# Second expert product of a four-layer network as seven half-size block products, with 32x64 tiles for the attention scores

## The chip, the cores and the metric

The kernel runs on one core of a Trainium2 chip. Its engines work side by side: PE (TensorE: matmuls, with PEld its weight loads), DVE (VectorE), ACT (ScalarE), POOL (GpSimd), and the queue SP, which here starts nearly all DMAs. Each follows its own instruction list in order, and they wait for each other on semaphores. The metric is device time in microseconds (us) of one execution; smaller is better.

## What is computed

Eight images (B = 8) of 512 tokens with 256 channels go through four layers. Each adds `s * silu(g)` to the running `x`, where `s` is an attention-like part and `g` a feed-forward part. Layer 0 has causal attention with 16 heads, layer 3 has two attentions, of which the second (over all tokens, 16 heads) uses the same class as layer 0's. In layer 1, which takes nearly half of the time, `s` is a state-space part with a convolution of four taps, and `g` a mixture of eight experts, all of them computed for every token:

```python
zxbcdt = u @ W_in.T                      # z, xBC, dt
xBC = silu(conv(xBC) + conv_b)           # four taps over time
y, _ = ssd(x * dt[..., None], A * dt, Bm, Cm, CHUNK)
y = (y + x * D).reshape(b, L, D_INNER) * silu(z)
s = rmsnorm(y) * norm_w @ W_out.T

gates = entmax_bisect(xt @ Wr + br)      # per token and expert
h = relu(einsum('td,edf->etf', xt, W1) + b1[:, None, :])   # 256 -> 1024
y = einsum('etf,efd->etd', h, W2) + b2[:, None, :]         # 1024 -> 256
g = silu(einsum('etd,te->td', y, gates))
```

All matmuls run in float32. The profile shows each of them as two records of a weight load and a matmul, one after the other.

## The kernel before

**Layer 1** (`layer1`, L967 on) goes over the 8 images and in each over 8 experts. For one expert the first product (`expert_in`) turns x into `hidden` (eight tiles of 128 features by 512 tokens). It is already done as seven block products of half size instead of eight (`PRODUCTS`, seven pairs of a bank "a" or "b" and a turn), 4 matmuls each with 256 moving columns, over four PSUM banks `hid`. The sums of weight blocks that this needs (`w1_sums`, S1 to S4) are made by POOL in `weight_sums`, the sums of inputs in `input_sums`, and ACT and DVE put the seven results together in `hidden` (`part_out`, `add_11`, `add_22`, `add_12`, `relus`). The second product (`expert_out`, L1203) is plain: for each of four token tiles j, eight matmuls add up over f into one of two banks `exp_out`, with 128 tokens of `hidden` as the stationary side and 256 columns of `w2` as the moving one, and DVE adds the result times the gate to `moe` (`expert_sum`, L1744). So an expert costs 56 records in `expert_in` and 64 in `expert_out`.

PE's order in an image is written by hand (`sequence`): the projections z0 to z3 and xb0 to xb3 (L1304), `expert_in(0)`, `expert_in(1)`, the gates, `expert_out(0)`, then `expert_in(e + 1)` and `expert_out(e)` in turn, with the state-space part in pieces between them (`cumulative`, `tokens`, `chunk_scores`, `chunk_products`), then `output` (L1296) and `expert_out(7)`. The projections and the state-space part share a ring of two banks, in the order of `names`; a bank can be written again when the engine that reads it is done (`Jobs.open` waits for `emptied`). ACT empties z0 to z3 (silu, L1428) and xb0 to xb3 (copy, L1364).

SP loads for every expert two halves of its first weights (`w1_first`, `w1_second`, 512 KB each) and its second weights (`w2`, 1 MB). `w1_second` and `w2` have two buffers each, so that load e + 2 starts when expert e is done with its own; `w1_first` has one.

**Attention** (class `Attention`, L285, used in layers 0 and 3): 16 heads, four at a time, each in its own 32 rows of the array. Every head's scores are computed twice, once for the row maxima (`score`, L387) and once transposed for the exponentials (`score_t`, L394), one matmul of 32 rows x 128 columns of weights for a tile of 128. `values` (L409) multiplies with four 128x32 tiles side by side. In a step PE runs score_t 0 and 1 and score 2 and 3, then the values, then score 0 and 1 and score_t 2 and 3. There are 128 steps in each of the two layers, with two such blocks of four score matmuls in each, so 512 blocks. In layer 0 a matmul has 512, 384, 256 or 128 moving columns (causal), in layer 3 always 512.

## Time and profile before

| | |
|---|---|
| median of 3 runs | 4200.58 us (4198.15 to 4203.7) |
| the profiled execution, its own time | 4203.91 us |
| its span in the trace | 4202.1 us |
| PE busy | 4062.9 us, 97% |
| PEld, DVE, ACT, POOL busy | 65%, 56%, 45%, 15% |
| mean granted TensorE clock | 0.986 of full |

A row of a timeline reads: start, length, engine, source line, operation, tile written and tiles read, shapes and count; in brackets how long the engine had been idle and who released it. A shape such as 32*128 is the weights' rows*columns, the shape after it what moves. A matmul's end is modelled, so the distance from start to start tells more than its length does. POOL, DVE, ACT and PE stand for the engines, SPq for the DMA queue of SP.

### The profile page before, as it was taken

The numbers are of one execution on the slowest core, as the hardware profiler recorded it, in microseconds if no ns is written. First come the engines' busy times: TensorE is split into PE (matmuls) and PEld (weight loads), VectorE is DVE, ScalarE is ACT, GpSimd is POOL, SyncE is SP. The second block draws the span as 40 slices with busy tenths as digits, with TensorE's granted clock in tenths as the row PEclk, the third lists the DMA queues.
The fourth block names the chain that finished last, engine by engine and source line by source line (L and its number), as shares of the span: only waits on it lengthen the run. The fifth ranks groups of instructions, "written<-read, shape, count | busy, mean of one in ns | idle before, by whom it ended". The sixth has DMA issues, their size and how long they took to land. (4 is left out here: it accounts for less than half of the span.)

```text
span 4202.1 us, 57679 instructions
## 1 busy us (share of the span) xinstructions
PE 4062.9 (97%) x21117; PEld 2729.2 (65%) x21117; DVE 2345.7 (56%) x4792; ACT 1888.4 (45%) x3783; POOL 646.7 (15%) x700
## 2 busy tenths in 40 slices
PE   7999999999999999999999999999998998999999
PEld 3444457888888888888888888666665554333333
DVE  6566655334343443434343343577777987667665
ACT  2454455435354444435444353455543221555555
POOL 0122123313133131323213131000000000000000
PEclk8999999999999999999999999999999999999999
DMA  3110102212122221222212121100000001011110
GB/s 90 17 17 16 34 12 99 80 61 98 65 85 79 71 88 61 88 71 87 82 61 88 66 97 47 47 1 1 1 1 22 1 1 26 16 24 21 26 24 22
DMA packets 61888, 198.51 MB, mean 47 GB/s; under 512 B 11257, under 2 KB 21121, under 8 KB 52745
## 3 DMA queue, kind: packets, MB, share of 16 engines
q1 hardware_dynamic: 60784, 194.55, 14.9%
q8 instruction: 172, 2.82, 0.3%
q14 instruction: 116, 0.94, 0.1%
q10 hardware_dynamic: 816, 0.20, 0.0%
HBM read 171.11 MB, written 4.46 MB: 42 GB/s over the span
## 5 line engine op out<-in xcount | busy, mean ns | idle before, releaser
L1211 PE MATMUL l_exp_out<-l_w,l_hidden 128*128 128x256 f32 x4096 | 913.6, 381 | 0.3
L1211 PEld LDWEIGHTS l_exp_out<-l_w,l_hidden 128*128 128x128 f32 x4096 | 769.0, 190 | 116.0 <-issue 9.1
L1369 ACT ACTIVATE l_hidden<-l_hid 128x512 f32<-128x512 f32 x384 | 227.7, 596 | 605.3 <-PE l_hid L1171 604.1
L1747 DVE SCALAR_TENSOR_TENSOR l_moe<-l_exp_out,l_gates,l_moe 128x256 f32<-128x256 f32 x256 | 123.8, 483 | 610.1 <-PE l_exp_out L1211 607.9
L1678 DVE TENSOR_TENSOR l_hidden<-l_hid,l_hidden 128x512 f32<-128x512 f32 x384 | 264.7, 691 | 348.2 <-PE l_hid L1171 343.7
L507 DVE TENSOR_REDUCE l3f_row_max<-l3f_bank 128x1 f32<-128x512 f32 x512 | 327.9, 685 | 176.9 <-PE l3f_bank L387 176.5
L463 ACT ACTIVATE l3f_prob_t<-l3f_bank 128x512 f32<-128x512 f32 x512 | 277.2, 596 | 206.1 <-PE l3f_bank L394 206.0
L1171 PE MATMUL l_hid<-l_x_sums,l_w_sums 128*128 128x256 f32 x1536 | 344.1, 381 | 7.4 <-DVE l_hidden L1678 7.4
L1171 PEld LDWEIGHTS l_hid<-l_x_sums,l_w_sums 128*128 128x128 f32 x1536 | 292.6, 191 | 47.6 <-issue 7.8
L504 DVE CUSTOM_DVE_ANT_0 l_masked<-l_bank,l_mask 128x256 f32<-128x256 f32 (+3 forms) x512 | 226.7, 487 | 161.0 <-PE l_bank L387 160.1
L1381 ACT ACTIVATE l_hidden<-l_hidden,l_w 128x256 f32<-128x256 f32 (+1 forms) x512 | 279.1, 605 | 65.2 <-DVE l_hidden L1678 64.8
L394 PE MATMUL l3f_bank<-l3f_qk_t 32*128 32x512 f32 x1024 | 302.9, 637 | 1.0 <-DMA l3f_qk_t<-l3f_set_rows 0.5
L387 PE MATMUL l3f_bank<-l3f_qk_t 32*128 32x512 f32 x1024 | 297.3, 643 | 5.4 <-DMA l3f_qk_t<-l3f_packed 5.2
L463 ACT ACTIVATE l_prob_t<-l_bank 128x256 f32<-128x256 f32 (+3 forms) x512 | 194.6, 436 | 208.4 <-PE l_bank L394 203.9
L1568 POOL TENSOR_TENSOR l_w_sums<-l_w_first,l_w_second 128x512 f32<-128x512 f32 x64 | 81.3, 1270 | 1116.4 <-PE l_hid L1171 1002.4
L394 PE MATMUL l_bank<-l_qk_t 32*128 32x512 f32 (+3 forms) x1024 | 217.8, 480 | 9.0 <-ACT l_prob_t L463 8.0
L387 PE MATMUL l_bank<-l_qk_t 32*128 32x512 f32 (+3 forms) x1024 | 217.1, 491 | 6.3 <-DMA l_qk_t<-in_alibi 5.5
L494 POOL TENSOR_SCALAR_AFFINE_SELECT l_prob_t<-l_prob_t 128x256 f32<-128x256 f32 x256 | 116.6, 457 | 502.0 <-ACT l_prob_t L463 501.6
L387 PEld LDWEIGHTS l3f_bank<-l3f_qk_t 32*128 32x128 f32 x1024 | 83.7, 183 | 97.5 <-issue 78.4
L409 PE MATMUL l3f_bank<-l3f_prob_t,l3f_v_ones 128*32 128x512 f32 x1024 | 138.1, 605 | 0.0
L394 PEld LDWEIGHTS l_bank<-l_qk_t 32*128 32x128 f32 x1024 | 92.1, 183 | 69.0 <-issue 44.7
L394 PEld LDWEIGHTS l3f_bank<-l3f_qk_t 32*128 32x128 f32 x1024 | 87.6, 183 | 75.1 <-issue 54.3
(525 smaller groups left out, 6779.3 us busy)
## 6 DMA issues: line engine op xcount, KB each, us to landing
l_w<-in_w SPq DMA_DIRECT2D x64, 1024.0 KB, 4.8
l_w_first<-in_w SPq DMA_DIRECT2D x64, 512.0 KB
l_w_second<-in_w SPq DMA_DIRECT2D x64, 512.0 KB, 3.7
l_mix<-l_cum SPq DMA_DIRECT2D x32, 512.0 KB, 4.8
l_qk_t<-l_packed SPq DMA_DIRECT2D x128, 64.0 KB
l3f_qk_t<-l3f_packed SPq DMA_DIRECT2D x128, 64.0 KB
all_x<-in_x SPq DMA_DIRECT2D x8, 512.0 KB, 6.0
out_x<-all_x SPq DMA_DIRECT2D x7, 512.0 KB, 3.0
```

Of the source, the lines that this page charges most:

```text
L387: flow.fill(nc.tensor.matmul(bank[:, 0:keys], self.q_t[rows, g, qt * P:(qt + 1) * P], self.k_t[rows, g, 0:keys], start=True, stop=True), ( ...
L394: flow.fill(nc.tensor.matmul(bank[:, 0:T - q.start], self.k_t[rows, g, kb * P:(kb + 1) * P], self.q_t[rows, g, q], start=True, stop=True), ...
L409: ins = nc.tensor.matmul(bank[self.rows(s), q], self.v[:, b % 2, kb, g * HPG + s, :], self.prob_t[:, u % (self.LAG + 1), s, 0:T - q.start] ...
L463: flow.empty(nc.scalar.activation(self.prob_t[:, t % (self.LAG + 1), s, 0:T - q.start], bank[:, 0:T - q.start], ACT.Exp), ("t", t, s))
L504: ins = nc.vector.tensor_tensor_reduce(self.masked[:, flow.index(("s", w, s)), 0:keys], bank[:, 0:keys], mask[:, T - keys:T], 1.0, NEG, AL ...
L507: ins = nc.vector.tensor_reduce(out, bank[:, 0:keys], AX, ALU.max)
L1171: ins = nc.tensor.matmul(bank[:, i * TH:(i + 1) * TH], weights[:, k * P:(k + 1) * P], moving, start=i == 0 and (which, turn) in (("a", 0), ...
L1211: ins = nc.tensor.matmul(bank[:, 0:C], hidden[:, e % 2, f, j * P:(j + 1) * P], w2[:, e % 2, f, :], start=f == 0, stop=f == HF - 1)
L1369: hid.empty(nc.scalar.activation(hidden_block(e, half_f, x, half_t), pair(bank), ACT.Copy), (e, x, which, turn))
L1381: return nc.scalar.activation(out, source, ACT.Relu, bias=w[:, B1][:, e * HF + k:e * HF + k + 1])
L1678: hid.empty(V.tensor_tensor(cell, pair(bank), cell, ALU.add), (e, x, which, turn))
L1747: exp_out.empty(V.scalar_tensor_tensor(moe[:, j, :], bank[:, 0:C], gates[:, j, e:e + 1], moe[:, j, :], ALU.mult, ALU.add), (e, j))
```

## The change

The second product of an expert now is seven block products too. Tokens, features and output columns are each cut in two; a product is 8 matmuls (2 token tiles x 4 feature tiles), still with 128 tokens of `hidden` stationary but with 128 moving columns of `w2`. Four sums of blocks of `w2` (R1, the one written over `w2_quarter(0, 1)`, R2, R4) are made by POOL (`w2_weight_sums`), four of `hidden` by DVE (`hidden_sum_1` to `hidden_sum_4`, one over `hidden_quarter(e, 1, 0)`, one over `hidden_quarter(e, 0, 1)`). The products go in turn to the two banks `exp_out` (a, b, a, b, a, b, a); some add to what the bank holds, and DVE adds each bank's state to `moe` after every product, so 14 operations of 128x128 for an expert take the place of 4 of 128x256.

`w1_second` and `w2` have one buffer now. The next expert's halves are loaded when the present expert is done with them, S3 is the first of the sums of `w1`, and S1, S2, S4 wait for the second half. The projections run xb0 to xb3 before z0 to z3. The convolution on DVE moves from `expert_out(0)` to the beginning of the image, among the additions of `expert_in(0)`. On ACT, Sqrt of the routing, Silu of `moe` and Exp and Ln of dt come between and behind the copies of xb and ahead of z. The routing is cut in pieces between the sums of expert 7.

In both attentions a score tile is computed as two matmuls of 32 rows x 64 columns of weights, into partitions 0 to 63 and 64 to 127 of the same bank, each with the same moving columns as before.

```diff
-            flow.fill(nc.tensor.matmul(bank[:, 0:keys], self.q_t[rows, g, qt * P:(qt + 1) * P], self.k_t[rows, g, 0:keys],
-                                       start=True, stop=True), ("s", w, s))
+            for m in range(0, P, 2 * SLOT):
+                ins = nc.tensor.matmul(bank[m:m + 2 * SLOT, 0:keys], self.q_t[rows, g, qt * P + m:qt * P + m + 2 * SLOT], self.k_t[rows, g, 0:keys],
+                                       start=True, stop=True)
+            flow.fill(ins, ("s", w, s))
...
-        w1_first, w1_second, w1_sums = a.sb("w1_first", [P, F]), a.sb("w1_second", [P, 2, F]), a.sb("w1_sums", [P, 4, HALF_F])
-        w2 = a.sb("w2", [P, 2, HF, C])
+        w1_first, w1_second, w1_sums = a.sb("w1_first", [P, F]), a.sb("w1_second", [P, F]), a.sb("w1_sums", [P, 4, HALF_F])
+        w2, w2_sums = a.sb("w2", [P, HF, C]), a.sb("w2_sums", [P, 3, HF // 2, P])
...
-                if not (is_last and e >= E - 2):
                     hid.wait_filled(sp, b, (e, 1, "a", 3))
-                    load_second((e + 2) % E)
+                    load_second((e + 1) % E)
...
-                    if not (is_last and e >= E - 2):
-                        exp_out.wait_filled(sp, b, (e, TJ - 1))
-                        load_w2((e + 2) % E)
+                    if not (is_last and e == E - 1):
+                        exp_out.wait_filled(sp, b, (e, "a", 3))
+                        load_w2((e + 1) % E)
...
+                def out_product(e, which, turn, tokens, weights, start):
+                    bank = exp_out.open(pe, b, (e, which, turn))
+                    for i in range(2):
+                        for k in range(HF // 2):
+                            ins = nc.tensor.matmul(bank[:, i * P:(i + 1) * P], tokens[:, k, i * P:(i + 1) * P], weights[:, k, :],
+                                                   start=start and i == 0 and k == 0, stop=True, skip_group_check=True)
+                    exp_out.fill(ins, (e, which, turn))
...
-                    for j in range(TJ):
-                        bank = exp_out.open(pe, b, (e, j))
-                        for f in range(HF):
-                            ins = nc.tensor.matmul(bank[:, 0:C], hidden[:, e % 2, f, j * P:(j + 1) * P], w2[:, e % 2, f, :],
-                                                   start=f == 0, stop=f == HF - 1)
-                        exp_out.fill(ins, (e, j))
+                    out_product(e, "a", 0, hidden_quarter(e, 0, 0), w2_quarter(0, 0), True)
...
+                    out_product(e, "b", 0, hidden_quarter(e, 0, 1), w2_quarter(1, 0), True)
...
+                    pe.wait_ge(hidden_summed, 4 * n + 3)
+                    pe.wait_ge(w2_summed, 4 * n + 3)
+                    out_product(e, "a", 1, hidden_sums[:, H2], w2_sums[:, R2], False)
+                    out_product(e, "b", 1, hidden_sums[:, H1], w2_sums[:, R1], True)
...
-                for name, weight in (("z", wz), ("xb", wx)):
+                for name, weight in (("xb", wx), ("z", wz)):
...
-                V.tensor_tensor(w1_sums[:, S1, :], high, second[:, HALF_F:F], ALU.add).then_inc(w1_summed, 1)
                 if n:
                     hid.wait_filled(pool, before, (last, 1, "a", 2))
                 V.tensor_tensor(w1_sums[:, S3, :], low, high, ALU.subtract).then_inc(w1_summed, 1)
-                pool.wait_ge(w1_summed, n * 4 + 1)
+                pool.wait_ge(second_loaded, 16 * (n + 1))
+                V.tensor_tensor(w1_sums[:, S1, :], high, w1_second[:, HALF_F:F], ALU.add).then_inc(w1_summed, 1)
+                pool.wait_ge(w1_summed, n * 4 + 2)
                 V.tensor_tensor(w1_sums[:, S2, :], w1_sums[:, S1, :], low, ALU.subtract).then_inc(w1_summed, 1)
...
+                def expert_sum(e, which, turn, half_t, half_c):
+                    bank = exp_out.wait_filled(dve, b, (e, which, turn))
+                    c = slice(half_c * P, (half_c + 1) * P)
+                    for i in range(2):
+                        j = 2 * half_t + i
+                        ins = V.scalar_tensor_tensor(moe[:, j, c], bank[:, i * P:(i + 1) * P], gates[:, j, e:e + 1], moe[:, j, c],
+                                                     ALU.mult, ALU.add)
+                    exp_out.empty(ins, (e, which, turn))
```

ACT at the beginning of the second image. `l_spread` is the routing's square root, `l_moe` the gate's silu, `l_u` Exp and Ln, `l_z_act` the silu of z, `l_xbc` the copy of xb. Before:

```order
L1508 ACTIVATE l_rms<-l_rms 128x4
L1418 ACTIVATE l_spread<-l_spread 128x32
L1428 ACT_TABLE_LOAD
L1428 ACTIVATE l_z_act<-l_bank 128x512 x4
L1433 ACTIVATE l_moe<-l_moe 128x1024
L1364 ACTIVATE l_xbc<-l_bank 128x512
L1436 ACT_TABLE_LOAD
L1436 ACTIVATE l_u<-l_u 128x32
L1364 ACTIVATE l_xbc<-l_bank 128x512
L1439 ACT_TABLE_LOAD
L1439 ACTIVATE l_u<-l_u 128x32
L1364 ACTIVATE l_xbc<-l_bank 128x512 x2
```

After:

```order
L1537 ACTIVATE l_rms<-l_rms 128x4
L1394 ACTIVATE l_xbc<-l_bank 128x512
L1448 ACTIVATE l_spread<-l_spread 128x32
L1460 ACT_TABLE_LOAD
L1460 ACTIVATE l_moe<-l_moe 128x1024
L1394 ACTIVATE l_xbc<-l_bank 128x512 x3
L1465 ACT_TABLE_LOAD
L1465 ACTIVATE l_u<-l_u 128x32
L1467 ACT_TABLE_LOAD
L1467 ACTIVATE l_u<-l_u 128x32
L1470 ACT_TABLE_LOAD
L1470 ACTIVATE l_z_act<-l_bank 128x512 x4
```

The silu of z0, which frees the ring's bank for z2, stood first and now stands behind the four copies of xb, four other activations and the loads of four activation tables (Silu, Exp, Ln, Silu again). Ahead of this image's first `l_z_act` one table was loaded before.

PE in an image, from the end of `expert_in(1)` to the beginning of `expert_in(2)`. Before:

```order
L1171 MATMUL l_hid<-l_xn_t,l_w_sums 128x256 x4
L1171 MATMUL l_hid<-l_x_sums,l_w_second 128x256 x4
L1232 MATMUL l_bank<-l_b,l_c_t 128x256 x4
L1211 MATMUL l_exp_out<-l_w,l_hidden 128x256 x32
L1171 MATMUL l_hid<-l_xn_t,l_w_first 128x256 x4
L1171 MATMUL l_hid<-l_xn_t,l_w_second 128x256 x4
```

After:

```order
L1183 MATMUL l_hid<-l_xn_t,l_w_sums 128x256 x4
L1183 MATMUL l_hid<-l_x_sums,l_w_second 128x256 x4
L1262 MATMUL l_bank<-l_b,l_c_t 128x256 x4
L1219 MATMUL l_exp_out<-l_w,l_hidden 128x128 x16
L1219 MATMUL l_exp_out<-l_w_sums,l_hidden_sums 128x128 x16
L1219 MATMUL l_exp_out<-l_w,l_hidden 128x128 x16
L1219 MATMUL l_exp_out<-l_w_sums,l_hidden 128x128 x8
L1183 MATMUL l_hid<-l_xn_t,l_w_first 128x256 x4
L1183 MATMUL l_hid<-l_xn_t,l_w_second 128x256 x4
L1183 MATMUL l_hid<-l_x_sums,l_w_sums 128x256 x12
```

32 matmuls of 256 columns became 56 of 128 columns.

SP at the beginning of the layer, the loads ahead of the loop. Before:

```order
L1069 DMA l_w_first<-in_w 128x1024
L1072 DMA l_w_second<-in_w 128x1024 x2
L1075 DMA l_w<-in_w 128x2048
L1124 DMA l_b<-in_b 8x256
L1075 DMA l_w<-in_w 128x2048
```

After:

```order
L1084 DMA l_w_first<-in_w 128x1024
L1087 DMA l_w_second<-in_w 128x1024
L1090 DMA l_w<-in_w 128x2048
L1137 DMA l_b<-in_b 8x256
L1138 UNCONDITIONAL_BRANCH
```

The second load of `w1_second` and the second of `w2` (`l_w` here) are gone: each expert's load now waits for the expert before.

DVE at the second product of expert 0 (the rows named ISA and REGISTER_ALU are waits). Before, the convolution's taps and the four sums into `l_moe` in turn (one round):

```order
L1747 SCALAR_TENSOR_TENSOR l_moe<-l_exp_out,l_gates,l_moe 128x256
L1757 SCALAR_TENSOR_TENSOR l_conv<-l_xbc,l_w,l_conv 128x512 x4
L1757 SCALAR_TENSOR_TENSOR l_conv<-l_xbc,l_w,l_conv 48x512
L46 REGISTER_ALU
L1747 SCALAR_TENSOR_TENSOR l_moe<-l_exp_out,l_gates,l_moe 128x256
```

After:

```order
L1842 SCALAR_TENSOR_TENSOR l_moe<-l_exp_out,l_gates,l_moe 128x128 x2
L97 REGISTER_ALU
L89 ISA
L1842 SCALAR_TENSOR_TENSOR l_moe<-l_exp_out,l_gates,l_moe 128x128 x2
L1750 ISA
L1751 TENSOR_TENSOR l_hidden<-l_hidden,l_hidden_sums 128x4x256
L1842 SCALAR_TENSOR_TENSOR l_moe<-l_exp_out,l_gates,l_moe 128x128 x2
L89 REGISTER_ALU
L1842 SCALAR_TENSOR_TENSOR l_moe<-l_exp_out,l_gates,l_moe 128x128 x2
L1738 ISA
L1739 TENSOR_TENSOR l_hidden_sums<-l_hidden 128x1024
```

The taps have gone from there, and sums of blocks of `hidden` stand between the additions to `moe`.

## Rows read from the trace of the kernel before

**Rows 1.** Page, head and part 5: busy us, mean ns, idle before.

```profile
PE 4062.9 (97%) x21117; PEld 2729.2 (65%) x21117; DVE 2345.7 (56%) x4792; ACT 1888.4 (45%) x3783; POOL 646.7 (15%) x700
...
L1211 PE MATMUL l_exp_out<-l_w,l_hidden 128*128 128x256 f32 x4096 | 913.6, 381 | 0.3
```

**Rows 2.** Busy time by stretch: layer 0, layer 1, second attention of layer 3.

```profile
core 0: us, PE busy (x) PEld busy (x) DVE busy (x) ACT busy (x) POOL busy (x), PEclk, DMA share, GB/s
0.00:640.00 640.00, 577.75 (x4067) 291.78 (x4068) 392.31 (x1367) 283.68 (x690) 116.82 (x260) 0.97 0.14 31
640.00:2650.00 2010.00, 1998.12 (x9839) 1665.68 (x9837) 817.18 (x1692) 877.09 (x1773) 529.92 (x440) 1.00 0.22 77
...
3533.00:4202.00 669.00, 653.15 (x3988) 249.34 (x3988) 438.13 (x813) 365.14 (x690) 0.00 (x0) 0.99 0.12 25
```

**Rows 3.** PE timeline: one `expert_out`, what follows, and an `expert_in`'s first product.

```profile
881.43 13.98 PE L1211 MATMUL l_exp_out<-l_w,l_hidden 128*128 128x256 f32 x64
...
895.25 5.31 PE L1304 MATMUL l_bank<-l_xn_t,l_w 128*128 128x512 f32 x12
...
908.98 1.89 PE L1171 MATMUL l_hid<-l_xn_t,l_w_first 128*128 128x256 f32 x8
910.71 1.46 PE L1171 MATMUL l_hid<-l_xn_t,l_w_second 128*128 128x256 f32 x6
```

**Rows 4.** PEld timeline: matmuls of 128 columns, the first load behind one of 256.

```profile
2723.52 1.08 PEld L2021 LDWEIGHTS l_bank<-l_q_t,l_k_t 128*128 128x128 f32 x8
2724.51 0.30 PEld L2021 LDWEIGHTS l_bank<-l_xn_t,l_w 128*128 128x128 f32 x2
```

**Rows 5.** PE timeline: eight records with 16 moving columns.

```profile
844.60 0.96 PE L1290 MATMUL l_bank<-all_cst,l_sum_sq 128*128 128x16 f32 x8
845.41 0.89 PE L1171 MATMUL l_hid<-l_xn_t,l_w_first 128*128 128x256 f32 x3
```

**Rows 6.** PE timeline, second attention: values, a block of scores, the next work.

```profile
3791.25 1.06 PE L409 MATMUL l3f_bank<-l3f_prob_t,l3f_v_ones 128*32 128x512 f32 x8
3792.24 0.70 PE L387 MATMUL l3f_bank<-l3f_qk_t 32*128 32x512 f32 x2
3792.26 0.70 PE L394 MATMUL l3f_bank<-l3f_qk_t 32*128 32x512 f32 x2
3792.78 0.59 PE L387 MATMUL l3f_bank<-l3f_qk_t 32*128 32x512 f32 x2
3792.79 0.59 PE L394 MATMUL l3f_bank<-l3f_qk_t 32*128 32x512 f32 x2
3793.31 1.99 PE L3187 MATMUL l3f_bank<-l3f_w,l3f_xn_t 128*128 128x256 f32 x8
```

**Rows 7.** Durations by line, ns min/median/max, first and last start: 128, 64, 32 weight columns.

```profile
L394 PE MATMUL l3f_bank<-l3f_qk_t x1024: 587/588/692, 3575.3 to 4181.7; 32*128 32x512 f32 x171
...
L1270 PE MATMUL l_bank<-l_mix,l_x_dt x512: 272/273/323, 742.4 to 2583.8; 128*64 128x128 f32 x171
...
L409 PE MATMUL l3f_bank<-l3f_prob_t,l3f_v_ones x1024: 592/605/617, 3581.5 to 4185.6; 128*32 128x512 f32 x171
```

**Rows 8.** PE timeline: the last product of `expert_in(1)` in the first image, then the biases.

```profile
682.91 1.89 PE L1171 MATMUL l_hid<-l_x_sums,l_w_second 128*128 128x256 f32 x8
684.73 1.99 PE L1232 MATMUL l_bank<-l_b,l_c_t 8*128 8x256 f32 x8
```

**Rows 9.** SP's queue there, and `w1_second`'s loads, issue to landing.

```profile
684.83 0.33 SPq L1072 DMA_DIRECT2D l_w_second<-in_w  x1
...
DMA to landing us min/median/max: 3.4/3.7/6.3
```

**Rows 10.** Groups of POOL and DVE by form: busy us, mean ns, idle before.

```profile
L1568 POOL TENSOR_TENSOR l_w_sums<-l_w_first,l_w_second 128x512 f32<-128x512 f32 x64 | 81.3, 1270 | 1116.4 <-PE l_hid L1171 1002.4 <-DMA l_w_first<-in_w 114.0
...
L1747 DVE SCALAR_TENSOR_TENSOR l_moe<-l_exp_out,l_gates,l_moe 128x256 f32<-128x256 f32 x256 | 123.8, 483 | 610.1 <-PE l_exp_out L1211 607.9
...
L1740 DVE TENSOR_TENSOR l_mix<-l_mix,l_cb 128x1024 f32<-128x1024 f32 x32 | 38.9, 1215 | 0.0
L1782 DVE TENSOR_TENSOR l_state<-l_state,l_bank 16x128 f32<-16x128 f32 x64 | 18.0, 281 | 1.2
```

**Rows 11.** ACT timeline, beginning of the second image.

```profile
897.17 0.60 ACT L1428 ACTIVATE l_z_act<-l_bank 128x512 f32<-128x512 f32 x1 [22.10 <-PE l_bank L1304]
...
902.81 1.05 ACT L1433 ACTIVATE l_moe<-l_moe 128x1024 f32<-128x1024 f32 x1
904.03 0.60 ACT L1364 ACTIVATE l_xbc<-l_bank 128x512 f32<-128x512 f32 x1 [0.17 <-PE l_bank L1304]
904.65 1.28 ACT L1436 ACT_TABLE_LOAD   x1
905.94 0.23 ACT L1436 ACTIVATE l_u<-l_u 128x32 f32<-128x32 f32 x1
```

**Rows 12.** PE timeline: two waits of about 2 us elsewhere.

```profile
2714.83 1.09 PE L2030 MATMUL l_bank<-all_cst,all_xn 128*128 128x128 f32 x8 [2.44 <-DVE all_xn L194]
...
3488.15 5.40 PE L2735 MATMUL l3a_bank<-l3a_value_prod,all_cst 128*128 128x512 f32 x8 [1.95 <-DVE l3a_value_prod L2985]
```

**Rows 13.** Busy time and granted clock (PEclk) around these two.

```profile
2714.00:2720.00 6.00, 5.17 (x18) 2.87 (x19) 5.86 (x16) 1.09 (x2) 0.00 (x0) 1.00 0.01 3
...
3486.00:3496.00 10.00, 7.52 (x28) 2.43 (x24) 9.97 (x10) 0.72 (x2) 0.00 (x0) 0.83 0.00 0
```

More of the change, by code:

```diff
@@ L393, in score_t @@
             bank = flow.open(pe, "score" if w >= n and s >= HPG // 2 else "score_t", ("t", t, s))
-            flow.fill(nc.tensor.matmul(bank[:, 0:T - q.start], self.k_t[rows, g, kb * P:(kb + 1) * P], self.q_t[rows, g, q],
-                                       start=True, stop=True), ("t", t, s))
+            for m in range(0, P, 2 * SLOT):
+                ins = nc.tensor.matmul(bank[m:m + 2 * SLOT, 0:T - q.start], self.k_t[rows, g, kb * P + m:kb * P + m + 2 * SLOT], self.q_t[rows, g, q],
+                                       start=True, stop=True)
+            flow.fill(ins, ("t", t, s))
         def values(u):
@@ L1046, in layer1 @@
         S1, S2, S3, S4 = range(4)
+        H1, H2 = range(2)
+        R1, R2, R4 = range(3)
         def rows_of(f):
@@ L1424, in silu @@
                     nc.scalar.activation(conv[:, f, :], conv[:, f, :], ACT.Silu).then_inc(conv_act, 1)
+                inner(0)
+                root(b)
+                if b:
+                    exp_out.wait_emptied_through(act, b - 1, [(E - 1, "b", 2), (E - 1, "a", 3)])
+                    nc.scalar.activation(moe[:, :, :], moe[:, :, :], ACT.Silu).then_inc(gate_ready, 1)
+                inner(1)
+                inner(2)
+                inner(3)
+                act.wait_ge(abs_ready, b + 1)
+                nc.scalar.activation(u[:, :, :], u[:, :, :], ACT.Exp).then_inc(act_step, 1)
+                act.wait_ge(act_step, b + 1)
+                nc.scalar.activation(u[:, :, :], u[:, :, :], ACT.Ln, bias=1.0).then_inc(log_ready, 1)
                 for f in range(FT):
@@ L1428, in sequence @@
                     jobs.empty(nc.scalar.activation(z_act[:, f, :], bank[:, :], ACT.Silu), f"z{f}")
-                if not b:
-                    root(0)
-                else:
-                    exp_out.wait_emptied_through(act, b - 1, [(E - 1, j) for j in range(TJ)])
-                    nc.scalar.activation(moe[:, :, :], moe[:, :, :], ACT.Silu).then_inc(gate_ready, 1)
-                inner(0)
-                act.wait_ge(abs_ready, b + 1)
-                nc.scalar.activation(u[:, :, :], u[:, :, :], ACT.Exp).then_inc(act_step, 1)
-                inner(1)
-                act.wait_ge(act_step, b + 1)
-                nc.scalar.activation(u[:, :, :], u[:, :, :], ACT.Ln, bias=1.0).then_inc(log_ready, 1)
-                inner(2)
-                inner(3)
                 first_parts(0)
@@ L1562, in weight_sums @@
                 low, high = w1_first[:, 0:HALF_F], w1_first[:, HALF_F:F]
-                second = w1_second[:, e % 2, :]
                 pool.wait_ge(first_loaded, 16 * (n + 1))
-                pool.wait_ge(second_loaded[e % 2], 16 * (n // 2 + 1))
-                if n:
-                    hid.wait_filled(pool, before, (last, 1, "b", 1))
-                V.tensor_tensor(w1_sums[:, S1, :], high, second[:, HALF_F:F], ALU.add).then_inc(w1_summed, 1)
                 if n:
@@ L1692, in begin @@
                     gate()
-                for e in range(2):
-                    add_11(it, e)
-                    add_22(it, e)
-                    if e == 1:
-                        bank = ring.wait_filled(dve, it, "gt")
-                        ring.empty(V.tensor_copy(gates_t, bank[0:E, :]), "gt")
-                    add_12(it, e)
+                ring.wait_emptied_through(dve, it, ["xb0", "xb1"])
+                conv_taps(st, 0, 1)
+                ring.wait_emptied_through(dve, it, ["xb2", "xb3"])
+                conv_taps(st, 2)
+                add_11(it, 0)
+                conv_taps(st, 3)
+                add_22(it, 0)
+                add_12(it, 0)
+                conv_taps(st, FT).then_inc(conv_ready, 1)
+                add_11(it, 1)
+                hidden_sum_1(it, 0)
+                hidden_sum_3(it, 0)
+                add_22(it, 1)
+                bank = ring.wait_filled(dve, it, "gt")
+                ring.empty(V.tensor_copy(gates_t, bank[0:E, :]), "gt")
+                add_12(it, 1)
+                hidden_sum_2(it, 0)
                 for n in range(2):
@@ L1827, in sequence @@
                         chunk_out(e - 2)
-                    for j in range(TJ):
-                        expert_sum(e, j)
-                        if (e, j) == (6, 1) and not is_last:
-                            route_sums(st, jobs, b)
+                    expert_sums(e)
                     if e == 4 and not is_last:
```

212 lines of the change are left out of this document (148 added, 64 removed).

## The prediction

> **What bounds the kernel now.** I read the page's head first: TensorE is busy 97% of the span, no other engine over 65% [rows 1]. Busy time is an average, so the split by stretch comes next: in layer 1, 2010 us, PE is busy for all but 12 us at full clock, while DVE and ACT have more than half of their time free [rows 2]. There every microsecond of PE's work is one of the kernel's. The second attention of layer 3 has 16 us of PE idle in 669; in layer 0 it is 62 of 640. So the sum below goes over what PE executes, and over new waits of PE. The largest group of all is the one that the change rewrites, L1211 [rows 1].
>
> **The second product: columns against weight loads.** One expert's 64 records of 256 columns take from 881.43 to 895.25, 0.2159 us each [rows 3]; 4096 of them are 884.3 us. Afterwards an expert has 56 matmuls, 112 records, of 128 columns: 12.5% fewer columns. But a record needs a fresh load of 128 weight columns either way, and with half the columns the load may become the limit. Two rows bound it. Eight loads of real matmuls with 128 columns start from 2723.52 on, the next one at 2724.51; the first distance stands behind a matmul of 256 columns (0.216), so seven take 0.774, 0.1106 us each [rows 4]. With only 16 moving columns seven records still need 0.111: 0.81 us, less a first distance of about 0.03 [rows 5]. So the load takes 0.111 us whatever moves, and the pace at 128 columns is that of the load. I take 0.1114, the upper of the two; 7168 records are then 798.5 us. The gain is **85.8 us** (0.1106 would give 91.5). An expert's second product falls from 13.82 to 12.48 us.
>
> The Trainium skill, page "TensorE: Matmul & The Clock Gate", section "LDWEIGHTS", has the time as the weight's columns divided by 1.2 ns, 107 ns for 128. The trace's 0.111 is a little longer, and the page's figure would give a gain of 117 us; the measured one is used.
>
> **Score tiles.** A block of four score matmuls (eight records, four at a time) takes from 3792.24 to 3793.31, 1.07 us [rows 6]. Its first records last 0.105 us longer than its second (692 against 587 ns), since their weights are loaded in plain sight after the array changed its tiling; with 64 weight columns the same difference is 0.051 (323 against 272), with 32 it is 0.025 [rows 7]. So tiles of 64 columns save 0.054 per block. Against that eight matmuls enter instead of four, each about 0.007 behind the other (four within 0.02 [rows 6]): the last is 0.028 later. The passes of 512 columns stay as long, since all eight tiles are different parts of the array. Net 0.026 x 512 blocks = **13.3 us**, if eight run at once as four do now. Lower bound of the gain: none; upper: 0.054 x 512 = 27.6. What eight at once cost no row shows; that is a rival below.
>
> **One buffer for w1_second: a new wait.** For experts 2 to 7 a second product of 12.5 us lies between one `expert_in` and the next, and hides the load and POOL's sums. `expert_in(1)` follows `expert_in(0)` at once. Its second half can be asked for only when `expert_in(0)` is through. SP issues such a load 0.2 us after the end of the last product (the biases start at 684.73 after it, less a tiling change of 0.1; the issue is at 684.83 [rows 8, 9]), and it lands 3.7 us later. Until then PE has only the first product, 1.73 us (908.98 to 910.71 [rows 3]). So it waits 4.0 - 1.7 = 2.3 us, and 0.1 for an uncovered weight load. Then the product b0 gives 1.73 us of work, while POOL makes S1 and then S2, 1.27 us each [rows 10]: another 0.9. With that **3.3 us per image, 26.4 us**. Landing at 3.4 or 6.3 us [rows 9] bounds it at 24 and 47.
>
> The one buffer of w2 is different: load 5 us, three sums 3.8. The shortest time between two second products is `output`, 6.9 us (32 records of 0.216), before expert 7; the first sums are needed only after two products more, 3.6 us. 10.5 against 8.9: nothing, 1.6 us of margin. POOL gets 5.1 us more work per expert and has the room [rows 2].
>
> **The ring at an image's beginning: a second wait.** From 895.25 to 908.98 the eight projections run without a gap at 1.716 us each, over two banks, and ACT empties each 0.2 us after it is full [rows 3, 11]. Now counted from the first xb (t = 0): ACT copies xb0 until 2.5, does the square root (until 2.7), loads the Silu table (1.28) and does `moe` (1.05) until 5.1, and only then xb1, until 5.7. xb3 needs that bank at 5.15: 0.65 us of wait. xb3 is full at 7.7, copied at 8.3. Then Exp and Ln, each with a table of 1.28 and 0.23 of work [rows 11], then Silu's table again: 8.3 + 1.5 + 1.5 + 1.3 = 12.6; silu of z0 until 13.2. z2 needs that bank at 11.0 (z0 and z1 have run by then): 2.3 us. Together **3.0 us per image, 24 us**. The bound below is nothing, if the tables are loaded in time that ACT spends waiting; above, 4 us per image.
>
> **DVE.** The additions to `moe` are 14 of 128x128 instead of 4 of 128x256. Rows bound one between 0.281 (16x128) and 0.483 (128x256) [rows 10]; I take 0.35, so 4.9 us, and four sums of `hidden` of 1024 elements at 1.215 as L1740, 4.9 us. That is 9.8 us within a product of 12.5 and 7.9 more per expert, 63 per image, for an engine that has 1190 us free over eight images [rows 2]: on average it fits (505 us in all). What decides is the handover: a bank comes back every 3.6 us, and within the 1.8 us of the other bank's product DVE must have read it. It takes 0.2 to notice and 0.7 for the pair; a sum of 1.2 ahead of it leaves 0.3 less than needed in the worst place and fits elsewhere. Behind the end of `chunk_products` and at expert 7 (routing in between) I count 0.1 to 0.25 us: about 0.4 per image, **3 us**. The convolution's taps (14 us of DVE from t = 9.6 on) end among the additions of `expert_in(0)`, which start at about t = 20: hidden.
>
> **The clock and the end.** The granted clock stayed at 1.00 (2.4 GHz) around a wait of 2.44 us, but around one of 1.95 it was 0.83 over 10 us, so 3.4 us at 1.2 GHz and 1.7 us lost [rows 12, 13]. There are now two waits of about 2.3 us per image. One in four of such losses is my choice: **7 us** (none: 0; all: 27). The last `moe` half goes through ACT and DVE before layer 2 can start: **1 us**.
>
> Sum: -85.8 - 13.3 + 26.4 + 24 + 3 + 7 + 1 = **-37.7 us**. The profiled execution took 4203.91 us by its own time, 3.3 above the median of 4200.58 and 1.8 above its span; it becomes 4166.2, and the median 4162.9, say **4163**.
>
> **Rivals.**
> *The waits don't come (4105).* ACT finds the tables in time, or the load overlaps more than I see. For it: ACT has slack in layer 1 [rows 2]; against it: `second_loaded` is a wait without any other cover in `expert_in(1)`, and ACT's order is strict. 4163 - 26 - 24 - 7 = 4106; halves of it lie between.
> *DVE's handovers bind (about 4230).* Seven times per expert PE and DVE pass a bank to each other, 448 times. If each cost 0.084 us, the gain is gone; that is the point from which it decides. At 0.15, +67. For it: four sums of 1.2 us now stand between the additions. Against: the slack above, and now DVE waits 610 us for PE there [rows 10].
> *Score tiles do not run eight at once (4354).* The second half of a slot shares its rows with the first. If the array holds only four, the second four begin when the first are in their second pass, and a block has three passes instead of two: 0.429 us more at 512 columns (1.716 / 4 [rows 3]) and 0.267 on average in layer 0, times 256 each: 110 + 68 = 178, and the 13 are lost. For it: no row shows more than four at once. Against: four tiles side by side that share all rows (L409) do start together, eight records in 0.99 us [rows 6]. The Trainium skill, "TensorE: Matmul & The Clock Gate", Part 3, says that a weight load overlaps with a running matmul only where the row group differs; by it the halves would follow each other. L409's rows, with one row group for all four, speak against that.
> *The change does not do what it says* is no case here: the instruction list has the 56 matmuls.
>
> **How the numbers follow.** Forecast 4163 (4125 to 4192): 0.58. The waits mostly don't come, below 4125: 0.17. Between 4192 and 4209: 0.06. DVE's handovers: 0.08. Score tiles: 0.11. Faster by over 0.2% (below 4192): 0.75; within 0.2%, about what a measurement of this kernel can tell from no change: 0.06; slower: 0.19. The range of 8 in 10 is 4112 to 4228: it leaves out the score tiles and the ends of the two neighbours.
>
> **What would show it.** Right: L1219 at 0.111 us per record, 12.5 us per expert; a block of scores at 1.04 us; PE idle of 2.3 and 0.9 us in each `expert_in(1)`, released by the DMA and by POOL; PE idle before xb3 and z2, released by ACT. Wrong: a pace above 0.12 (each 0.01 costs 72 us), PE idle inside `expert_out` released by DVE, or score blocks of 1.4 us and more.

## The result

The changed kernel takes 4230.06 us (median of 3 runs, 4228.84 to 4237.71) against 4200.58 before: ratio 1.0075, 95% interval 1.0052 to 1.0098. It is 29.5 us slower, where 4163 was forecast. The profiled execution took 4237.7 us, its span is 4236.0.

### The profile page after: what moved, and what is told of

It is laid out like the page before. It is cut to its first block and busy times, and to the rows that moved or that the text cites. A ratio compares the mean times of both kernels' runs of the same rounds, so it can differ in the third digit from the quotient of the medians.

```text
span 4236.0 us, 73833 instructions
## 1 busy us (share of the span) xinstructions
PE 4000.2 (94%) x28285; PEld 2721.1 (64%) x28285; DVE 2936.9 (69%) x5688; ACT 1886.9 (45%) x3782; POOL 1119.1 (26%) x956
## 5 line engine op out<-in xcount | busy, mean ns | idle before, releaser
L1219 PE MATMUL l_exp_out<-l_w,l_hidden 128*128 128x128 f32 x4096 | 482.4, 276 | 0.5 <-DMA l_w<-in_w 0.5
L1219 PEld LDWEIGHTS l_exp_out<-l_w,l_hidden 128*128 128x128 f32 x4096 | 468.6, 192 | 10.8 <-issue 9.1
L1726 DVE TENSOR_TENSOR l_hidden<-l_hid,l_hidden 128x512 f32<-128x512 f32 x384 | 261.9, 690 | 236.6 <-PE l_hid L1183 231.8
L1842 DVE SCALAR_TENSOR_TENSOR l_moe<-l_exp_out,l_gates,l_moe 128x128 f32<-128x128 f32 x896 | 271.2, 344 | 215.6 <-PE l_exp_out L1219 188.1
L397 PE MATMUL l3f_bank<-l3f_qk_t 32*64 32x512 f32 x2048 | 293.7, 611 | 1.0 <-ACT l3f_prob_t L467 0.5
L388 PE MATMUL l3f_bank<-l3f_qk_t 32*64 32x512 f32 x2048 | 287.1, 616 | 5.3 <-DMA l3f_qk_t<-l3f_packed 5.2
L1219 PE MATMUL l_exp_out<-l_w_sums,l_hidden_sums 128*128 128x128 f32 x2048 | 242.9, 277 | 6.4 <-DVE l_moe L1842 6.4
L1219 PEld LDWEIGHTS l_exp_out<-l_w_sums,l_hidden_sums 128*128 128x128 f32 x2048 | 233.6, 192 | 10.8 <-issue 7.7
L397 PE MATMUL l_bank<-l_qk_t 32*64 32x512 f32 (+3 forms) x2048 | 206.0, 452 | 10.2 <-ACT l_prob_t L467 10.2
L388 PE MATMUL l_bank<-l_qk_t 32*64 32x512 f32 (+3 forms) x2048 | 206.0, 461 | 6.4 <-DMA l_qk_t<-in_alibi 5.5
L1603 POOL TENSOR_TENSOR l_w_sums<-l_w 128x512 f32<-128x512 f32 x64 | 87.2, 1362 | 464.4 <-DMA l_w<-in_w 464.4
L1595 POOL TENSOR_TENSOR l_w_sums<-l_w_first,l_w_second 128x512 f32<-128x512 f32 x64 | 82.8, 1294 | 375.7 <-DMA l_w_second<-in_w 375.7
L1183 PE MATMUL l_hid<-l_x_sums,l_w_second 128*128 128x256 f32 x512 | 133.4, 408 | 35.8 <-DVE l_hidden L1726 35.8
```

Of the source, the lines that this page charges most:

```text
L388: ins = nc.tensor.matmul(bank[m:m + 2 * SLOT, 0:keys], self.q_t[rows, g, qt * P + m:qt * P + m + 2 * SLOT], self.k_t[rows, g, 0:keys], sta ...
L397: ins = nc.tensor.matmul(bank[m:m + 2 * SLOT, 0:T - q.start], self.k_t[rows, g, kb * P + m:kb * P + m + 2 * SLOT], self.q_t[rows, g, q], s ...
L1183: ins = nc.tensor.matmul(bank[:, i * TH:(i + 1) * TH], weights[:, k * P:(k + 1) * P], moving, start=i == 0 and (which, turn) in (("a", 0), ...
L1219: ins = nc.tensor.matmul(bank[:, i * P:(i + 1) * P], tokens[:, k, i * P:(i + 1) * P], weights[:, k, :], start=start and i == 0 and k == 0, ...
L1726: hid.empty(V.tensor_tensor(cell, pair(bank), cell, ALU.add), (e, x, which, turn))
L1842: ins = V.scalar_tensor_tensor(moe[:, j, c], bank[:, i * P:(i + 1) * P], gates[:, j, e:e + 1], moe[:, j, c], ALU.mult, ALU.add)
```

## The profile after

The head of the page, then busy time by stretch (layer 0, layer 1, layer 2 with the first attention of layer 3, the second attention), of the changed kernel. The columns are those of [rows 2]:

```profile
PE 4000.2 (94%) x28285; PEld 2721.1 (64%) x28285; DVE 2936.9 (69%) x5688; ACT 1886.9 (45%) x3782; POOL 1119.1 (26%) x956
```

```profile
0.00:632.40 632.40, 565.99 (x6112) 263.20 (x6112) 392.12 (x1367) 283.59 (x690) 116.93 (x260) 0.98 0.14 31
632.40:2691.80 2059.40, 1954.09 (x12912) 1712.45 (x12912) 1408.60 (x2588) 876.08 (x1772) 1002.21 (x696) 0.98 0.22 75
2691.80:3573.40 881.60, 833.41 (x3226) 522.49 (x3226) 698.05 (x921) 362.37 (x630) 0.00 (x0) 0.98 0.02 9
3573.40:4236.00 662.60, 646.69 (x6036) 222.98 (x6036) 438.16 (x813) 364.83 (x690) 0.00 (x0) 0.99 0.13 25
```

PE's work did shrink: busy 4062.9 before [rows 1], 4000.2 now. But in layer 1, where PE was busy for all but 12 us of 2010 [rows 2], it now stands idle for 105. DVE's busy time there went from 817 to 1409 us, POOL's from 530 to 1002.

I split both traces by the distance from one piece of PE's work to the next. "Expected" is from the prediction:

| us | before | after | difference | expected |
|---|---|---|---|---|
| layer 0 | 639.4 | 632.4 | -7.0 | -6.65 |
| layer 1: `expert_out` (8 x 8) | 903.3 | 830.6 | -72.7 | -82.8 |
| layer 1: the eight projections (x 8) | 110.2 | 147.9 | +37.7 | +24 |
| layer 1: `expert_in(0)` and `(1)` up to the gates | 165.8 | 195.4 | +29.6 | +26.4 |
| layer 1: `expert_in(3)` | 97.4 | 147.1 | +49.7 | 0 |
| layer 1: the rest | 734.7 | 738.4 | +3.7 | +8 (clock, end) |
| layer 2, first attention of layer 3 | 882.1 | 881.6 | -0.5 | 0 |
| second attention of layer 3 | 669.1 | 662.6 | -6.6 | -6.65 |

One row stands out, and the prediction has nothing for it: `expert_in(3)`. Who held PE up in layer 1 (waits in us in total, times, longest):

```profile
PE l_hid L1183 <- DVE l_hidden L1726: 43.4, 9, 7.6
PE l_bank L1334 <- ACT l_z_act L1470: 17.8, 8, 2.2
PE l_hid L1183 <- DMA l_w_second<-in_w: 16.9, 8, 2.2
PE l_bank L1334 <- ACT l_xbc L1394: 8.7, 8, 7.2
PE l_exp_out L1219 <- DVE l_moe L1842: 7.8, 10, 1.5
...
PE l_hid L1183 <- POOL l_w_sums L1597: 2.8, 4, 0.7
```

The second, third and last line are the waits that were forecast: 2.2 us for z2 in each image, 2.1 for the load (forecast 2.3 each), and POOL's sum. The first is new: once per image 4.5 us of wait in `expert_in(3)` (and one of 7.6 in the last image, which stood there before, with 7.4). PE waits for an addition on DVE. So the next view is what DVE did in this time, and POOL beside it; second image, DVE's, POOL's and PE's timelines:

```profile
995.75 1.27 DVE L1726 TENSOR_TENSOR l_hidden<-l_hid,l_hidden 128x512 f32<-128x512 f32 x2
996.95 6.99 DVE L1880 TENSOR_TENSOR l_x_dt<-l_x_dt,l_dt 128x512 f32<-128x512 f32 x2
1004.15 1.98 DVE L1832 TENSOR_TENSOR l_mix<-l_mix,l_cb 128x1024 f32<-128x1024 f32 x1 [0.22 <-DVE l_x_dt L1880]
1006.06 0.68 DVE L1834 TENSOR_TENSOR l_x_dec<-l_x_dt,l_decays 128x512 f32<-128x512 f32 x1
```

```profile
995.25 2.78 POOL L1571 TENSOR_TENSOR l_c_scaled<-l_c_scaled,l_c_t 16x1024 f32<-16x1024 f32 x1
998.00 1.26 POOL L1603 TENSOR_TENSOR l_w_sums<-l_w 128x512 f32<-128x512 f32 x1
999.23 1.26 POOL L1604 TENSOR_TENSOR l_w<-l_w 128x512 f32<-128x512 f32 x1
1000.46 1.25 POOL L1606 TENSOR_TENSOR l_w_sums<-l_w,l_w_sums 128x512 f32<-128x512 f32 x1
1001.79 1.60 POOL L1608 TENSOR_TENSOR l_w_sums<-l_w,l_w_sums 128x512 f32<-128x512 f32 x1
```

```profile
1007.39 3.54 PE L1183 MATMUL l_hid<-l_x_sums,l_w_second 128*128 128x256 f32 x8 [4.48 <-DVE l_hidden L1726]
```

Two time steps (L1880, `time_step`) took 6.99 us together; 0.67 is what one needs. DVE shows as busy, but it stands still: POOL had begun before it and went from one instruction to the next without a pause, from 995.25 to 1001.71. The durations by line tell which of DVE's operations suffer (ns, min/median/max):

```profile
L1880 DVE TENSOR_TENSOR l_x_dt<-l_x_dt,l_dt x32: 673/1661/5325, 738.1 to 2523.3; 128x512 f32<-128x512 f32 x32
...
L1834 DVE TENSOR_TENSOR l_x_dec<-l_x_dt,l_decays x32: 678/1759/1765, 753.2 to 2617.1; 128x512 f32<-128x512 f32 x32
...
L1726 DVE TENSOR_TENSOR l_hidden<-l_hid,l_hidden x384: 673/692/694, 669.0 to 2651.8; 128x512 f32<-128x512 f32 x192
...
L1842 DVE SCALAR_TENSOR_TENSOR l_moe<-l_exp_out,l_gates,l_moe x896: 334/343/353, 701.4 to 2686.9; 128x128 f32<-128x128 f32 x180
```

L1726 and L1842 read one operand from PSUM (`hid`, `exp_out`); none of their 1280 operations took over 6% more than the shortest, though hundreds lie beside POOL's work. L1880 and L1834 read both from SBUF. The row that said so before the change was there to be read, in the durations of the kernel before:

```profile
L1763 DVE TENSOR_TENSOR l_x_dt<-l_x_dt,l_dt x32: 678/870/2552, 726.8 to 2475.6; 128x512 f32<-128x512 f32 x32
```

The same operation on the same tile, 0.68 to 2.55 us. The Trainium skill, page "SBUF — State Buffer", section "SBUF: two separate sides", has the rule: a VectorE operation with two SBUF inputs and a GpSimd operation that reads SBUF need the same pair of ports, whoever starts first holds it for the whole instruction, and the other stands. The trace agrees, by the four rows above, with one exception: eight of the 32 time steps lay beside POOL's L1584, which had started first and reads `conv` in SBUF, and took 673 to 683 ns. No run tells why that one holds nothing up.

## Experiments: who holds DVE up in `expert_in(3)`?

Two theories. A: POOL's work holds DVE up. B: DVE has too much in a row, since two of the four time steps moved from ahead of `expert_in(3)` to behind its first addition. The runs were timed beside the kernel before, whose medians there were 4199.6 to 4200.8.

**The sums of w2 cut to 8 columns.** One of the four sums:

```diff
-                V.tensor_tensor(w2_sums[:, R1], w2_quarter(0, 1), w2_quarter(0, 0), ALU.subtract).then_inc(w2_summed, 1)
+                V.tensor_tensor(w2_sums[:, R1, 0:1, 0:8], w2_quarter(0, 1)[:, 0:1, 0:8], w2_quarter(0, 0)[:, 0:1, 0:8], ALU.subtract).then_inc(w2_summed, 1)
```

> The changed kernel with POOL's four sums of w2 blocks over 8 columns instead of 512 each, so about 5 us less of POOL per expert; the rest of the sums is left out, which makes the second products wrong in value and nothing else. In the changed kernel PE waits 4.5 us in every expert_in(3) for DVE's addition, and DVE's time steps (L1880, 0.67 us at best) take up to 5.3 us while POOL works. Theory A, DVE is held up by POOL's work: time steps back at 0.7 to 1.7 us, expert_in(3) at 12.2 to 13 us instead of 18.4, 45 to 50 us less, about 4183. Theory B, DVE has simply too many operations in a row there since the time steps moved behind the first addition: durations and waits as they are, 4230.

Measured 4180.5 us, ratio to before 0.9952 (0.9936 to 0.9969). Layer 1 is 2008.3 us instead of 2059.4, `expert_in(3)` 12.2 to 12.9. DVE's list is unchanged, so theory B alone is out: in the same order, without these four sums beside it, DVE is in time. The time steps are still held by POOL's other work (674/952/2847 ns, where I had expected 1.7 us at most), but not long enough to make an addition late.

**Writes instead of sums.**

```diff
-                V.tensor_tensor(w2_sums[:, R1], w2_quarter(0, 1), w2_quarter(0, 0), ALU.subtract).then_inc(w2_summed, 1)
+                V.memset(w2_sums[:, R1], 0.0).then_inc(w2_summed, 1)
```

> The changed kernel with each of POOL's four sums of w2 blocks turned into a write of zeros over the same 128x512 elements, so POOL writes but reads nothing there (the sums are left out, the values are wrong). If what holds DVE up is POOL's reading: as with the sums cut short, about 4183, with DVE's durations at their minimum beside these writes. If any POOL work of this length holds it up: L1880 up to 3 us and more still, about 4230 less what the writes are shorter than 1.26 us.

Measured 4181.6, ratio 0.9960 (0.9948 to 0.9971). The time alone doesn't tell reading from length: POOL's memset of 128x512 took 0.52 us, not 1.26, so POOL was also busy for 3 us less per expert. The durations do:

```profile
L1834 DVE TENSOR_TENSOR l_x_dec<-l_x_dt,l_decays x32: 681/684/686, 736.4 to 2554.5; 128x512 f32<-128x512 f32 x32
```

In both traces 23 of these 32 lie beside POOL's instructions for w2 alone, of which one had started first. Beside the sums they took 1755 to 1765 ns, beside two or three memsets 682 to 686. Eight time steps beside memsets alone took 677 or 678. So POOL's writes alone held nothing up here.

**The time steps ahead of `expert_in(3)` again.**

```diff
                 sixth_sum(1)
                 time_step(0)
+                time_step(1)
+                time_step(2)
                 last_sum(1)
                 hidden_sum_2(b, 2)
-                time_step(1)
+                time_step(3).then_inc(x_dt_ready, 1)
...
-                        time_step(2)
-                        time_step(3).then_inc(x_dt_ready, 1)
```

> The changed kernel with the four time steps all ahead of expert_in(3), as in the kernel before, still reading and writing SBUF. If the place of two of them behind the first addition of expert_in(3) is what costs 6.2 us per image: expert_in(3) at 12.2, 4182. If DVE is held wherever POOL is busy: the time steps are stretched in their new place too, their sum stays at 40 us and more over the layer, and DVE comes to expert_in(3) late by some of it; chunk_mix (L1832, L1834) is still held there: 4195 to 4230.

Measured 4202.9, ratio 1.0005 (0.9994 to 1.0016): 27 us of the 50. In their new place 26 of the 32 time steps lie beside L1584 and nothing else of POOL's, and none of these was held (674 to 686 ns). So my "wherever POOL is busy" was too wide: it depends on what POOL does. But `expert_in(3)` is still 12.6 to 16.2 us long, because the next operations with two SBUF inputs now meet POOL's sums:

```profile
L1880 DVE TENSOR_TENSOR l_x_dt<-l_x_dt,l_dt x32: 674/682/1576, 737.9 to 2483.8; 128x512 f32<-128x512 f32 x32
...
L1834 DVE TENSOR_TENSOR l_x_dec<-l_x_dt,l_decays x32: 685/1757/4052, 749.9 to 2582.8; 128x512 f32<-128x512 f32 x32
```

So the place has its part: it decides how many held operations stand between two additions that PE waits for. Without POOL's sums the place costs nothing, with them more than half.

**The time steps from PSUM.** They read the bank that PE filled, ACT's copies into SBUF go, and the steps move up into `expert_out(1)`, since the ring needs its banks:

```diff
-                    jobs.wait_emptied(dve, b, f"xk{j}")
-                    return V.tensor_tensor(heads(x_dt[:, j, :]), heads(x_dt[:, j, :]), per_head(dt[:, j, :]), ALU.mult)
+                    bank = jobs.wait_filled(dve, b, f"xk{j}")
+                    jobs.empty(V.tensor_tensor(heads(x_dt[:, j, :]), heads(bank[:, :]), per_head(dt[:, j, :]), ALU.mult), f"xk{j}")
```

> The changed kernel with the four time steps reading their tile from PSUM instead of from ACT's copy in SBUF; ACT's four copies go, and the time steps stand within expert_out(1). In the changed kernel DVE's operations with one PSUM input never take more than 4% over their shortest, beside POOL or not. Theory A: each at 0.7 us, no wait of PE in expert_in(3), 4180 to 4185. The rest of DVE's operations with two SBUF inputs (sums of hidden, L1832, L1834) stays stretched. If the time steps now delay the additions of expert_out(1), up to 1 us per image of it comes back, 4190.

Measured 4197.6, ratio 1.0001 (0.9991 to 1.0011).

```profile
L1876 DVE TENSOR_TENSOR l_x_dt<-l_bank,l_dt x32: 678/681/692, 722.8 to 2471.0; 128x512 f32<-128x512 f32 x32
```

The operand decides: not one of 32 was held, though 16 of them lay beside POOL's sums of `w1`, of the kind beside which L1751 took up to 2.30 us instead of 1.22 in the changed kernel. My 4180 to 4185 was too low for the same reason as above: `chunk_mix` is held instead (its L1828 takes 1.99 us on average, L1830 1.72). In five of the eight images one L1828 takes 5.7 us, and in the same five `expert_in(3)` is 14.2 us.

## Experiments: the projections and the score tiles

**The order of the projections undone.** z before xb, with ACT's order of before and each tap waiting for its xb:

```diff
-                for name, weight in (("xb", wx), ("z", wz)):
+                for name, weight in (("z", wz), ("xb", wx)):
```

> The changed kernel with the projections and ACT's work on them in the order of the kernel before (z0 to z3, then xb0 to xb3; square root, Silu of moe, Exp and Ln between the copies of xb), and the convolution's taps waiting for each xb. The eight projections took 110 us over all images before and 148 in the changed kernel, of which the first image has 13. If ACT's order is the cause: 110 to 112 again, 36 to 38 us less, 4192 to 4194, if the taps, now 7 us later on DVE, cost nothing; if they hold up the first additions of expert_in(0), up to 2.4 us per image back, at most 4212. If the order isn't the cause: 148 and 4230.

Measured 4234.1, ratio 1.0078 (1.0051 to 1.0104), no gain at all. The projections do come back to 114.1 us, so ACT's order is what they had lost by. But `expert_in(0)` and `(1)`, up to the gates, grew from 24.4 to 28.4 us per image:

```profile
914.00 1.89 PE L1183 MATMUL l_hid<-l_x_sums,l_w_sums 128*128 128x256 f32 x8
918.17 5.38 PE L1183 MATMUL l_hid<-l_x_sums,l_w_sums 128*128 128x256 f32 x16 [2.28 <-DVE l_hidden L1729]
```

The taps start later and DVE's first addition comes 2.3 us too late; the rest is clock (granted 0.68 from 918.2 to 923.6, so 1.7 us lost; more on this below). The order with xb first pays 3 us per image to save about as much.

**z between `expert_in(0)` and `expert_in(1)`**, with ACT's and DVE's orders made to match; PE's part:

```diff
+                projections("xb", wx)
                 expert_in(0)
+                projections("z", wz)
                 expert_in(1, {5: gates_in})
```

> The changed kernel with the projections z0 to z3 between expert_in(0) and expert_in(1), Exp and Ln behind expert_in(1) on ACT, and DVE's taps, gate and sums placed to match. The load of w1_second and POOL's sums then have 6.9 us of PE work above them. Expected: projections 110 to 112 us (38 less), no waits for the DMA and POOL in expert_in(1) (3.3 us per image, 26 less): 4166. The wait of 6.2 us per image in expert_in(3) stays. If DVE is late with its additions to expert_in(0) or (1), DVE shows as the releaser there, and each us per image costs 8.

Measured 4218.8, ratio 1.0046 (1.0031 to 1.0061). Layer 1 is 2034.4 us. The projections take 110.6, and the waits for `w1_second` and for POOL's sum are gone, both as expected. In layer 1 that is 25 us of the 64 forecast, mostly because `expert_in(0)` now takes 14.7 to 16.5 us instead of 12.1 from the second image on. DVE's timeline there shows six taps, `conv_taps(st, 0, 1)`, that need 4.3:

```profile
898.72 8.14 DVE L1773 SCALAR_TENSOR_TENSOR l_conv<-l_xbc,l_w,l_conv 128x512 f32<-128x512 f32 x6
```

The taps have two SBUF inputs too, and met POOL's sums in their new place. Of the 25 us only 11 are left in the median. In the profiled execution the second attention of layer 3, the same code as in the changed kernel, took 674 us instead of 663, at a granted clock of 0.966 instead of 0.987; what lowered it, no run tells.

**Both.** The last two together:

> z_between and step_from_psum together. Each took its own wait away and they touch different places, so the gains should add: 4230 - 64 - 33 = 4133. If a wait stands behind the other one (DVE late by the same amount elsewhere), less than the sum: 4145 or more.

Measured 4167.5, ratio 0.9924 (0.9894 to 0.9954), 34 us above the sum that I had expected. Both leave POOL's sums beside DVE: over the eight images `expert_in(0)` is 24 us and `expert_in(3)` 10 us longer than in the kernel before.

**The score tiles alone**, in the kernel before:

> The kernel before with the 32x64 score tiles alone. By the traces layer 0 is 7.0 us and the second attention of layer 3 6.6 us shorter in the changed kernel: 4187. If part of that came from anything else in the change, less: 4190 to 4200.

Measured 4186.6, ratio 0.9969 (0.9957 to 0.9982): 13.0 us less. Eight tiles do run at once. A block in the changed kernel, with the values ahead of it and the next work behind:

```profile
3804.02 1.06 PE L413 MATMUL l3f_bank<-l3f_prob_t,l3f_v_ones 128*32 128x512 f32 x8
3805.01 0.66 PE L388 MATMUL l3f_bank<-l3f_qk_t 32*64 32x512 f32 x4
3805.04 0.66 PE L397 MATMUL l3f_bank<-l3f_qk_t 32*64 32x512 f32 x4
3805.49 0.61 PE L388 MATMUL l3f_bank<-l3f_qk_t 32*64 32x512 f32 x4
3805.52 0.61 PE L397 MATMUL l3f_bank<-l3f_qk_t 32*64 32x512 f32 x4
3806.06 1.99 PE L3312 MATMUL l3f_bank<-l3f_w,l3f_y_t 128*128 128x256 f32 x8
```

The first eight records start together, the second eight half a microsecond later: two passes and not three, 1.05 us against 1.07 [rows 6].

## Experiments: a version without the collision

**The sums made once.** z_between, and POOL makes the sums of w2 in the first image only. SP stores them in DRAM and loads them in the other seven:

```diff
+            def load_kept(e):
+                sp.dma_start(w2[:, :, :], w2_kept[e]).then_inc(w2_loaded, 16)
+                sp.dma_start(w2_sums[:, :, :, :], w2_sums_kept[e]).then_inc(w2_sums_loaded, 16)
...
             def w2_weight_sums(n):
+                if n >= E:
+                    return
```

> z_between, and the sums of w2 blocks are made by POOL in the first image only, stored in DRAM and loaded from there in the other seven (1.75 MB per expert instead of 1 MB). The time steps are as in the changed kernel. If POOL's work is what holds DVE in expert_in(3): seven eighths of 50 us less than z_between, 4120 to 4125. If the longer loads (about 8 us for both instead of 4.8) or the stores in the first image hold PE up, DMA shows as releaser in expert_out: 4130 and more.

Measured 4137.6, ratio 0.9854 (0.9826 to 0.9882). This run holds its own control, since from `expert_in(2)` on PE's and DVE's lists are alike in every image: `expert_in(3)` took 18.6 us in the first image, with POOL's sums, and 12.18 in each of the other seven, without. The six taps are back at 4.32:

```profile
898.30 4.32 DVE L1799 SCALAR_TENSOR_TENSOR l_conv<-l_xbc,l_w,l_conv 128x512 f32<-128x512 f32 x6
```

The load of 1.75 MB per expert held nothing up. The 13 to 18 us over my forecast are in the first image (`expert_in(0)` to `expert_out(0)`, 10 us more than in the second) and in `expert_in(1)`, 1.1 us in each later image, where the sums of `hidden` stand ahead of an addition.

**Tuned.** That and the time steps from PSUM, the first addition of `expert_in(1)` ahead of the sums of `hidden`, and the 28 statistics of layer 2's norm, for which PE waited 7.4 us in the last image of the kernel before as well, in four pieces:

> sums_kept and step_from_psum together, and two smaller moves on DVE: the first addition of expert_in(1) ahead of the sums of hidden, and in the last image the statistics of layer 2's norm in four pieces instead of one of 11 us. Waits left in sums_kept by its trace: 6.4 us in the first image's expert_in(3), 1.1 us in each later expert_in(1), 10.8 us in the last image's expert_in(6). If they go: 4137.6 - 5 - 7.6 - 10 = 4115; if DVE's pieces come late elsewhere, up to 4130.

Measured 4115.7 (4105.8 to 4118.3), ratio 0.9804 (0.9788 to 0.9821): 84 us faster than the kernel before, 114 faster than the changed one. Layer 1, again with its columns as in [rows 2]:

```profile
626.10:2559.50 1933.40, 1917.20 (x12912) 1697.89 (x12912) 1330.54 (x2588) 862.00 (x1741) 695.08 (x472) 1.00 0.31 111
```

PE is busy for all but 16 us of 1933. About 10 us of the 84 come from the split statistics, which the kernel before could have had too.

## Why the prediction was wrong, step by step

- **The pace was right.** An expert's second product runs from 890.97 to 903.47, as forecast 12.5 us; 0.1116 us a record against 0.1114.

```profile
890.97 3.73 PE L1219 MATMUL l_exp_out<-l_w,l_hidden 128*128 128x128 f32 x32
...
901.68 1.95 PE L1219 MATMUL l_exp_out<-l_w_sums,l_hidden 128*128 128x128 f32 x16
903.47 5.32 PE L1334 MATMUL l_bank<-l_xn_t,l_w 128*128 128x512 f32 x12
```

- **POOL at no price: the step that failed.** "POOL gets 5.1 us more work per expert and has the room." It had, and took the room from DVE. I counted each engine's free time by itself. By the rows, L1880 lost 52 us over its 32 operations (73.9 busy, 0.673 each at best) against 12 before (34.1 busy), and 16 with the sums of w2 cut. The new sums of `hidden` lost some 60, but with the sums of w2 cut as well: POOL's older work holds them, and PE hardly waits for it. What stood between two additions of `expert_in(3)` was not hidden: 49.7 us. That alone is more than the whole gain of 37.7 that I had forecast.
- **The rival at "about 4230": its number, not its mechanism.** The median is 4230.06, but that is chance. By that rival 448 handovers in `expert_out` cost 0.084 us each; they cost 11.6 us together, 0.026 each, and 49.7 us came in `expert_in(3)`, of which it says nothing.
- **The time steps: an edit not priced.** The order shows two of them behind `add_11` of `expert_in(3)`, and the prediction doesn't speak of it. It costs nothing by itself (pool_sums_cut) and 27 us together with POOL (steps_early).
- **DVE's handover in `expert_out`: right mechanism, too small.** By its pace the second product gains 84.3 us (64 x 12.50 against 884.3), of which 11.6 come back in and between its parts instead of 3. PE's waits for DVE, 7.8 us, mostly 0.9 at `expert_out(0)`, are most of that.
- **The ring: right for a later image, wrong for the first.** Images 2 to 8 lose 3.0 us as worked out (16.74 against 13.73 us; 0.4 ahead of xb3 instead of 0.65, 2.5 ahead of z2 instead of 2.3), with 1.7 more in two of them (clock). The first loses 13.3. There ACT's square root, ahead of the copy of xb1, waits until DVE has done the whole routing, which itself began only at 640.8:

```profile
650.80 0.23 ACT L1448 ACTIVATE l_spread<-l_spread 128x32 f32<-128x32 f32 x1 [8.44 <-DVE l_spread L1697]
...
651.56 7.39 PE L1334 MATMUL l_bank<-l_xn_t,l_w 128*128 128x512 f32 x12 [7.16 <-ACT l_xbc L1394]
```

I took "does the square root (until 2.7)" from an image whose routing was long done, and multiplied by eight.
- **`w1_second`: right.** 2.1 us for the load and 0.7 for POOL, 29.6 us over the layer against 26.4. The 2.3 was added up 0.1 too high: 0.2 until the issue and 3.7 until the landing, less 1.7, are 2.2. Most of the rest is that four images went on at a lower clock behind the wait.
- **The clock.** Of the waits of 2.2 us for z2, two in eight are followed by 1.7 us of loss, so one in four was close for these. Of the eight waits for the load four are followed by a loss, but of only 0.5 us each, since the slower product behind them also fills the wait for POOL (granted 0.61 from 682.2 to 685.2). But after the wait of 4.5 us the loss came in every image. Busy times from the wait on, with the granted clock third from last:

```profile
1002.90:1007.40 4.50, 0.02 (x2) 0.01 (x1) 4.28 (x5) 0.03 (x1) 2.15 (x2) 0.97 0.00 0
1007.40:1013.00 5.60, 5.60 (x39) 4.27 (x39) 2.60 (x5) 5.57 (x12) 0.00 (x0) 0.72 0.21 42
```

  The product behind it takes 3.47 us instead of 1.73: 1.2 GHz. So 4.5 us of wait cost 6.2.
- **Score tiles: right in the attention of layer 3**, where 6.6 us went (forecast 6.65). Timed alone they gave 13.0 of 13.3. That layer 0 gave 7.0 is in part luck: with the same code it took from 626.1 to 632.7 us in the eleven traces that have these tiles (granted clock 0.97 to 0.98), so 6.7 to 13.3 less than before. The rival with three passes is out.

The misses add up: -37.7 + 49.7 (`expert_in(3)`) + 13.7 (projections) + 10.1 (second product) + 3.2 (`expert_in(0)` and `(1)`) - 5.1 (the rest) = +33.9, the difference of the two spans.

## What to carry over

Before work goes to an idle POOL, list what DVE does beside it and where its operands lie: each operation with two SBUF inputs can be held, and it shows as a long duration, not as idle time. So compare a line's shortest duration with its median and longest, before pricing anything by its mean. Give the operand in PSUM to DVE where there is a choice, and make sums of weights once if they are used again.
